# A decoder's expert stage: other blocks of batches, and another pacing of the gathers that merge the experts' outputs

## The chip, the core and the metric

The kernel runs on one core of one Trainium2 chip. The metric is the device time of one execution in microseconds; the median of several executions counts. Engines: TensorE (PE: matrix products and transposes; PEld: its weight loads), VectorE (DVE), ScalarE (ACT), GpSimd (POOL), and SyncE (SP), which here only issues DMAs. GpSimd issues the indirect DMAs (gathers and scatters by row numbers) itself. All DMAs run on the core's 16 DMA engines.

## The reference, cut to what matters

A decoder of two layers over 32 batches of 256 tokens of width 256. Layer 0 and the attention and cross attention of layer 1 come first; the change lies in the last part, the experts of layer 1. Each token is normalised, scored against 8 experts, and gets the sum of its two best experts' outputs, each times its score, added to the residual.

```python
scores = xf @ gate_w + gate_b
topk_s, topk_i = jax.lax.top_k(scores, 2)
comb = zeros.at[arange(n)[:, None], topk_i].add(topk_s)
h = jnp.maximum(einsum('nd,edh->neh', xf, w1) + b1, 0.0)
eo = einsum('neh,ehd->ned', h, w2) + b2
out = einsum('ne,ned->nd', comb, eo)          # then added to the residual x5
```

The kernel computes for each token only its two experts, not all eight.

## The kernel before

The program is a row of phases with a barrier of all engines between them. The last two matter here.

**Cross pass with routing** (`cross_pass`). A software pipeline of slots; in slot n batch n-3 is routed. `file_rows` on GpSimd scatters each normalised row twice into `expert_in`, into the region of its expert. The batches are cut into three blocks (`Dispatch.BLOCKS`: 15, 10 and 7 batches). In each block the rows of one expert are padded to whole tiles of 256 rows, so a block of n batches has 2n + 7 tiles (`Dispatch.tiles`: 37, 27, 21; 85 in all). When the last batch of a block has been routed, DVE makes its tables (`tables`, L2098 to L2139, 20 small operations, each waiting for the one before): which expert and which rows each tile has, and `out_slots`, where each token finds its two results. SP then stores the zero rows of the padding (`pad`). In slots 18, 23, 28 and 33 DVE also makes the low part of a quarter of the expert weights (L2145).

**Expert stage** (`experts_phase`). One tile is 256 rows of one expert. All products are made in fp32r in three passes (high times low, low times high, high times high). For tile m, the loop iteration m on TensorE is: `hT(m)`, transposes of the hidden layer; `xT(m + 2)`, transposes of the input; `up(m + 1)`, the up product, 12 matmuls; `down(m)`, the down product, 12 matmuls. ACT takes the high parts (`x_high`, `h_high`), DVE the low parts and the biases (`x_low` d_xl, `add_b1` d_up, `h_low` d_hl, `add_b2` d_eo). The evacuation d_eo(m) is what DVE does as soon as `down(m)` is done. SP loads d_xs five tiles ahead and stores d_eo into `expert_out` of the block.

**Merging.** When all of a block's tiles are in memory, its batches can be merged. For each batch GpSimd issues four gathers of 128 rows (L2368, d_pick, a ring of four: gather b waits until batch b - 4 is summed), ACT multiplies them by the scores (`weight`, L2393, four operations), DVE adds the two (L2445) and the residual (L2449), and SP stores the result. A gather would otherwise run ahead, so `gather_at` paces the gathers: it counts in halves of a tile, and the gather at half h waits for `up(h // 2)` if h is even, for `down(h // 2)` if it is odd. So there are two gathers a tile and a batch in two tiles; gathers at or behind half 170 (tile 85, the number of tiles) wait for no product. `ready_after` says after which tile a batch's weighting stands in ACT's program; its adds stand one tile later in DVE's, behind that tile's d_eo. Each engine works in the order of its program.

Semaphores count: `xT_psum`, `up_psum` and `out_psum` say how many tiles have their input transposes, up product and down product done; `eo_stored` says what is in memory.

Of the kernel before, what the change touches and what calls it, by code (L numbers as in the profile page):

```python
# [68 lines left out]
def stand_alone(eng, passed):  # L69

    eng.sem_inc(passed, 1)


class Steps:
# [6 lines left out]
    def __init__(self, eng, sem, each, before=0):  # L81
        self.eng, self.sem, self.each, self.before, self.base, self.n = eng, sem, each, before, 0, 0
# [14 lines left out]
def make_identity(nc, tile, ready, before):  # L97

    nc.gpsimd.memset(tile[:, :], 0.0).then_inc(ready, 1)
    nc.gpsimd.wait_ge(ready, before + 1)  # L100
    nc.gpsimd.affine_select(out=tile[:, :], in_=tile[:, :], compare_op=ALU.not_equal, fill=1.0, base=0,
                            pattern=[[-1, P]], channel_multiplier=1).then_inc(ready, 1)
# [1007 lines left out]
class Dispatch:  # L1110


    def __init__(self, nc, ctx, B, S, NE, D):
        T = S // P
        sb = lambda name, shape, dt=F32: ctx.enter_context(nc.sbuf_tensor("e_" + name, shape, dt))
        self.BLOCKS = (B // 2 - 1, B // 4 + 2, B // 4 - 1)
        self.NE, self.TILE = NE, 2 * P
        most = max(self.BLOCKS) * S
        self.region = most + self.TILE
        self.stride = NE * self.region + (NE - 1) * self.TILE  # L1120
        self.tiles = [2 * n * S // self.TILE + NE - 1 for n in self.BLOCKS]
        self.base = [k * self.stride for k in range(len(self.BLOCKS))]
        rows = len(self.BLOCKS) * self.stride
        self.xs_d = nc.dram_tensor("expert_in", (rows, D), F32).ap()
        self.eo_d = [nc.dram_tensor(f"expert_out{k}", (n * self.TILE, D), F32).ap() for k, n in enumerate(self.tiles)]
        self.x5_d = nc.dram_tensor("x5_scratch", (B * S, D), F32).ap()
        self.slots = sb("slots", [P, B, T, 2], I32)
        self.coef = sb("coef", [P, B, T, 2])
        self.ixf, self.pos = sb("ixf", [P, B, T, 2]), sb("pos", [P, B, T, 2])
        self.out_slots = sb("out_slots", [P, B, T, 2], I32)  # L1130
        self.row = [sb(f"row{k}", [P, n], I32) for k, n in enumerate(self.tiles)]
        self.expert = [sb(f"expert{k}", [P, n], I32) for k, n in enumerate(self.tiles)]
# [25 lines left out]
def phase_c(nc, a, x3_d, out, w):  # L1158

    B, S, D = a["ctx_1024"].shape  # L1160
    with ExitStack() as ctx:
        ex = Dispatch(nc, ctx, B, S, a["L1_ffn_gate_w"].shape[1], D)
        x4_d = nc.dram_tensor("x4_scratch", (B * S, D), F32).ap()
        with nc.cleanup_on_exit():
            attention_pass(nc, a, x3_d, x4_d, w)
        nc.all_engine_barrier()
        ex.weights(nc, ctx, a)
        with nc.cleanup_on_exit():
            cross_pass(nc, a, x4_d, w, ex)
        nc.all_engine_barrier()  # L1170
        experts_phase(nc, out, ex, D)
# [1084 lines left out]
def experts_phase(nc, out, ex, D):  # L2256

    NE = ex.NE
    C, T = D // P, ex.TILE // P
    B = sum(ex.BLOCKS)  # L2260
    ROWS = ex.xs_d.shape[0]
    TILES = [(k, j) for k, n in enumerate(ex.tiles) for j in range(n)]
    N = len(TILES)
    XR, ER, GR = 6, 3, 4
    with ExitStack() as ctx:  # L2265
# [20 lines left out]
        xT_psum, xT_high, xT_ready = sem("xT_psum"), sem("xT_high"), sem("xT_ready")  # L2286
        up_psum, up_ready = sem("up_psum"), sem("up_ready")
        hT_psum, hT_high, hT_ready = sem("hT_psum"), sem("hT_high"), sem("hT_ready")
        out_psum, eo_ready = sem("out_psum"), sem("eo_ready")
# [7 lines left out]
        first = [sum(ex.tiles[:k]) for k in range(len(ex.tiles))]  # L2297
        gather_at, pace = [], 0
        for k, n in enumerate(ex.BLOCKS):
            pace = max(pace, 2 * (first[k] + ex.tiles[k] + 1))  # L2300
            for b in range(n):
                gather_at.append(range(pace, pace + 2 * T))
                pace += 2 * T
        ready_after = [min(N, at[-1] // 2 + 2) for at in gather_at]
        merged_after = lambda m: [b for b in range(B) if ready_after[b] == m]

        block = ctx.enter_context(nc.Block())
# [1 line left out]
        @block.sync  # L2309
        def _(sync):  # L2310
            def load(m):
                k, j = TILES[m]
                row = sync.value_load(ex.row[k][0:1, j:j + 1], min_val=0, max_val=ROWS - ex.TILE)  # L2313
                if m >= XR:
                    sync.wait_ge(xT_psum, m - XR + 1)
                sync.dma_start(xs[m % XR][:, :, :], ex.xs_d[bass.ds(row, ex.TILE), :]
                               .rearrange("(t p) d -> p t d", p=P)).then_inc(xs_loaded[m % XR], 16)

            def store(m):
                k, j = TILES[m]  # L2320
                sync.wait_ge(eo_ready, m + 1)
                sync.dma_start(ex.eo_d[k][j * ex.TILE:(j + 1) * ex.TILE, :].rearrange("(t p) d -> p t d", p=P),
                               eo[m % ER][:, :, :]).then_inc(eo_stored[m % ER], 16)

            def load_x5(b):
                if b >= GR:
                    sync.wait_ge(summed, b - GR + 1)
                sync.dma_start(x5[b % GR][:, :, :], x5_rows[b]).then_inc(x5_loaded[b % GR], 16)

            def store_out(b):  # L2330
                sync.wait_ge(summed, b + 1)
                sync.dma_start(out_rows[b], y[b % 2][:, :, :]).then_inc(out_stored[b % 2], 16)

            for m in range(XR - 1):
                load(m)
            for b in range(GR):
                load_x5(b)
            for m in range(N + 1):
                if m + XR - 1 < N:
                    load(m + XR - 1)  # L2340
                if m < N:
                    store(m)
                for b in merged_after(m - 1) + merged_after(N) * (m == N):
                    store_out(b)
                    if b + GR < B:
                        load_x5(b + GR)
            for u in range(2):
                sync.wait_ge(out_stored[u], 16 * (B // 2))

        @block.gpsimd  # L2350
        def _(pool):
            g = nc.gpsimd
            make_identity(nc, ident, consts, 0)
            b = 0
            for k, n in enumerate(ex.BLOCKS):
                done = first[k] + ex.tiles[k]
                for r in range(ER):
                    pool.wait_ge(eo_stored[r], 16 * len([m for m in range(done) if m % ER == r]))
                for _ in range(n):
                    if b >= GR:  # L2360
                        pool.wait_ge(summed, b - GR + 1)
                    stand_alone(pool, pool_passed)
                    for t in range(T):
                        for c in range(2):
                            half = gather_at[b][2 * t + c]
                            if half // 2 < N:
                                pool.wait_ge((up_psum, out_psum)[half % 2], half // 2 + 1)
                            g.indirect_dma_start(pick[b % GR][:, t, c, :], None, ex.eo_d[k],  # L2368
                                                 bass.IndirectOffsetOnAxis(ap=ex.out_slots[:, b, t, c:c + 1], axis=0),
                                                 bounds_check=ex.eo_d[k].shape[0] - 1, oob_is_err=False).then_inc(picked[b % GR], 16)  # L2370
                    b += 1
# [202 lines left out]
```

## Time and profile before

| | us |
|---|---|
| median of 3 runs | 2791.55 |
| lowest, highest | 2788.91, 2796.89 |
| profiled execution | 2796.21 |
| its span, first to last instruction | 2794.4 |
| mean granted TensorE clock, share of full | 0.937 |

The profile is of one execution. A row of the timeline gives start, duration, engine, line, operation, output and inputs, and in brackets how long the engine sat idle before and what ended that. A row of the windows gives start and end, length, each engine's busy time with its count of instructions, then the granted TensorE clock, the busy share of the DMA engines and GB/s. The releaser named by a bracket is inferred: of several waits it is the one that ended last. Matmuls overlap, so their starts are 0.12 us apart though each shows 0.28. Idle time of an engine that nothing waits for costs nothing.

### The profile page before, as it was taken

What the parts mean: (1) busy time and instruction counts of PE and PEld (TensorE: products, weight loads), DVE (VectorE), ACT (ScalarE), POOL (GpSimd) and SP (SyncE); (2) the same over time, 40 slices, a digit from 0 to 9 for tenths busy, and PEclk for the clock granted to TensorE, in tenths of its full rate; (3) what the DMA queues carried; (4) which work ended last, traced back from release to release, by engine and by line L of the source; (5) the groups of instructions that cost most, each with busy time, mean ns of one, the idle gap of its engine ahead of it and who ended that gap; (6) DMA issues with size and microseconds to landing.
All of it is one profiled execution on the core that took longest, in us unless ns stands there. A gap on an engine that the chain in (4) does not pass through costs nothing. (4 is left out here: it accounts for less than half of the span.)

```text
span 2794.4 us, 49866 instructions
## 1 busy us (share of the span) xinstructions
PE 2401.1 (86%) x16388; PEld 1884.8 (67%) x16388; DVE 1893.6 (68%) x4393; ACT 1515.3 (54%) x3016; POOL 1359.5 (49%) x1313
## 2 busy tenths in 40 slices
PE   5999999479999668999999999887998987799991
PEld 3666666369999645656656566555887776799981
DVE  3888888456565347777777777754777775567773
ACT  3777777345555336776767676662433432223443
POOL 4677777444443254554545545402665555002556
PEclk9999999789999878999999999997999998899996
DMA  2222221252121001111111111114332433445885
GB/s 66 66 77 61 76 76 50 60 146 96 66 74 52 25 18 37 37 42 41 41 41 38 43 43 37 33 35 137 102 121 99 155 111 108 156 139 186 256 249 179
DMA packets 234395, 242.72 MB, mean 87 GB/s; under 512 B 34670, under 2 KB 220272, under 8 KB 233888
## 3 DMA queue, kind: packets, MB, share of 16 engines
q1 hardware_dynamic: 212576, 193.14, 22.6%
q0 software_dynamic: 20480, 46.39, 5.5%
q8 instruction: 138, 2.26, 0.4%
q14 instruction: 113, 0.93, 0.2%
q10 hardware_dynamic: 1088, 0.00, 0.0%
HBM read 133.82 MB, written 101.25 MB: 84 GB/s over the span
## 5 line engine op out<-in xcount | busy, mean ns | idle before, releaser
L1527 DVE TENSOR_REDUCE f_nm<-f_raw 128x4 f32<-128x1024 f32 x256 | 312.8, 1222 | 108.5 <-PE f_raw L1641 105.7
L1353 POOL TENSOR_TENSOR f_hm<-f_hm,f_mhalf 128x64 f32<-128x64 f32 x32 | 366.4, 11449 | 2.7
L1420 ACT ACTIVATE f_PT<-f_sco 128x1024 f32<-128x1024 f32 x256 | 262.2, 1024 | 97.3 <-PE f_sco L1658 97.2
L2368 POOL DMA_INDIRECT d_pick<-expert_out,e_out_slots x128 | 141.0, 1102 | 255.4 <-DMA expert_out<-d_eo 154.4
L910 ACT ACTIVATE b_hT<-b_H,b_b1r 128x512 f32<-128x512 f32 x128 | 88.2, 689 | 163.5 <-PE b_H L1039 148.1
L1658 PE MATMUL f_sco<-f_q4T,f_k4T 64*128 64x256 f32 x1024 | 130.6, 335 | 50.1 <-DMA f_q4T<-f_nmT 35.6
L2387 ACT ACTIVATE d_hh<-d_H 128x512 fp32r<-128x512 f32 x85 | 50.8, 598 | 205.2 <-PE d_H L2473 205.2
L1895 POOL DMA_INDIRECT expert_in<-g_xm,e_slots x128 | 131.0, 1024 | 40.2 <-issue 37.0
L677 PE MATMUL a_bank<-a_w,a_xnT 128*128 128x512 f32 x256 | 127.0, 620 | 21.9 <-ACT a_xnT L394 21.9
L1054 PE MATMUL b_O<-b_w2l,b_hTh 128*128 128x256 f32 x512 | 144.9, 283 | 0.0
L1054 PE MATMUL b_O<-b_w2h,b_hTl 128*128 128x256 f32 x512 | 144.7, 283 | 0.0
L1054 PE MATMUL b_O<-b_w2h,b_hTh 128*128 128x256 f32 x512 | 144.7, 283 | 0.0
L864 POOL DMA_INDIRECT x_scratch<-b_y,b_idx x64 | 69.2, 1082 | 144.6 <-DVE b_y L987 128.7
L1658 PEld LDWEIGHTS f_sco<-f_q4T,f_k4T 64*128 64x128 f32 x1024 | 82.4, 198 | 84.6 <-DMA f_q4T<-f_nmT 42.6
L1641 PE MATMUL f_raw<-f_k4T,f_q4T 64*128 64x256 f32 x1024 | 131.3, 336 | 6.9 <-DVE f_nm L1527 5.2
L1351 POOL TENSOR_SCALAR f_hm<-f_hm 128x64 f32<-128x64 f32 x32 | 32.4, 1014 | 204.4 <-DVE f_hm L1491 204.4
L972 DVE TENSOR_TENSOR b_hTl<-b_hT,b_hTh 128x512 fp32r<-128x512 f32 x128 | 88.2, 690 | 61.4 <-ACT b_hTh L912 57.5
L1641 PEld LDWEIGHTS f_raw<-f_k4T,f_q4T 64*128 64x128 f32 x1024 | 81.7, 197 | 56.0 <-issue 41.2
L2493 PE MATMUL d_O<-e_w2l,d_hh 128*128 x340 | 98.4, 289 | 13.5 <-DVE d_hl L2430 13.5
L1344 POOL TENSOR_SCALAR f_rs<-f_mv 128x2 f32<-128x2 f32 x32 | 7.0, 220 | 205.8 <-DVE f_mv L1477 205.8
L1039 PE MATMUL b_H<-b_xTh,b_w1l 128*128 128x512 f32 x256 | 102.5, 400 | 2.5 <-DVE b_xTl L957 2.5
L2493 PE MATMUL d_U<-e_w1l,d_xh 128*128 x340 | 104.0, 306 | 0.1
(367 smaller groups left out, 7758.8 us busy)
## 6 DMA issues: line engine op xcount, KB each, us to landing
d_xs<-expert_in SPq DMA_DIRECT2D x85, 256.0 KB
expert_out<-d_eo SPq DMA_DIRECT2D x85, 256.0 KB
x_scratch<-a_x SPq DMA_DIRECT2D x64, 256.0 KB, 2.2
b_w<-in_L_ffn_W_dram SPq DMA_DIRECT2D x16, 1024.0 KB
a_x<-in_x_dram SPq DMA_DIRECT2D x32, 256.0 KB
a_cx<-in_ctx_dram SPq DMA_DIRECT2D x32, 256.0 KB
f_x<-x_scratch SPq DMA_DIRECT2D x32, 256.0 KB
f_q4T<-f_nmT SPq DMA_DIRECT2D x128, 64.0 KB, 2.3
```

Of the source, the lines that this page charges most:

```text
L677: last = t_.matmul(bank_of(part)[:, :], xnT[b % 2][:, c, t * P:(t + 1) * P], w[:, c, 0:2 * D], start=c == 0, stop=c == C - 1)
L910: s.activation(hT[f % 4][:, :], HB[f % 4][:, :], ACT.Gelu, bias=b1r[:, e, f:f + 1], scale=RATIO).then_inc(hidden, 1)
L1039: last = t_.matmul(HB[f % 4][:, :], w[e % 2][:, c, cols], x[:, c, :], start=m == 0, stop=m == len(products) - 1)
L1054: last = t_.matmul(OB[t // 2][:, t % 2 * D:(t % 2 + 1) * D], h[:, f, cols], w[e % 2][:, f, :], start=f == 0 and m == 0, stop=f == FC - 1 a ...
L1353: g.tensor_tensor(hm[b % 2][:, :], hm[b % 2][:, :], mhalf[:, :], ALU.pow).then_inc(hroot, 1)
L1420: s.activation(PT[n % 3][:, t, :, :], heads(SCO), ACT.Exp, scale=float(DH) ** -0.5).then_inc(probs_ready, 1)
L1527: v.tensor_reduce(nm[:, t, g * HG:(g + 1) * HG], heads(RAW), AX.X, ALU.max, negate=True)\
L1641: last = t_.matmul(heads(RAW)[:, place(h), :], q4T[b % 3][at, h // 2, t * P:(t + 1) * P], k4T[b % 3][at, h // 2, :], start=True, stop=True)
L1658: last = t_.matmul(heads(SCO)[:, place(h), :], k4T[b % 3][at, h // 2, t * P:(t + 1) * P], q4T[b % 3][at, h // 2, :], start=True, stop=True)
L1895: g.indirect_dma_start(ex.xs_d, bass.IndirectOffsetOnAxis(ap=ex.slots[:, b, t, k:k + 1], axis=0), xm[b % 3][:, t, :], None, bounds_check=e ...
L2368: g.indirect_dma_start(pick[b % GR][:, t, c, :], None, ex.eo_d[k], bass.IndirectOffsetOnAxis(ap=ex.out_slots[:, b, t, c:c + 1], axis=0), b ...
L2493: last = t_.matmul(halves(bank)[:, t, :], x[:, c, t * P:(t + 1) * P], y_[:, bass.ds(e, 1), c, :].rearrange("p o d -> p (o d)"), start=c == ...
```

## The change

The blocks become 18, 9 and 5 batches, with 43, 25 and 17 tiles, again 85. The pacing counts in sixths of a tile. In block 0 gathers are two sixths apart, three a tile, so a batch takes 4/3 of a tile; in the other blocks three sixths apart, two a tile, as before. The first sixths of tile m now wait for `xT(m + 2)`, the middle ones for `up(m + 1)`, the last for `down(m)`: all three are of loop iteration m. From tile 84 on there is no wait for a product. Block 0's gathers begin at tile 44 (before: at half 76, tile 38), block 1's at tile 69, and block 2's follow when the last tile is stored. All line numbers behind L2297 grow by one.

```diff
-        self.BLOCKS = (B // 2 - 1, B // 4 + 2, B // 4 - 1)
+        self.BLOCKS = (B // 2 + 2, B // 4 + 1, B // 8 + 1)
...
         for k, n in enumerate(ex.BLOCKS):
-            pace = max(pace, 2 * (first[k] + ex.tiles[k] + 1))
+            each = 2 if k == 0 else 3
+            pace = max(pace, 6 * (first[k] + ex.tiles[k] + 1))
             for b in range(n):
-                gather_at.append(range(pace, pace + 2 * T))
-                pace += 2 * T
-        ready_after = [min(N, at[-1] // 2 + 2) for at in gather_at]
+                gather_at.append(range(pace, pace + 2 * T * each, each))
+                pace += 2 * T * each
+        ready_after = [min(N, at[-1] // 6 + 2) for at in gather_at]
...
-                            half = gather_at[b][2 * t + c]
-                            if half // 2 < N:
-                                pool.wait_ge((up_psum, out_psum)[half % 2], half // 2 + 1)
+                            m, sixth = divmod(gather_at[b][2 * t + c], 6)
+                            if m + 1 < N:
+                                pool.wait_ge(*((xT_psum, min(N, m + 3)), (up_psum, m + 2), (out_psum, m + 1))[sixth // 2])
```

The start of the gathers in GpSimd's program, before. Semaphores are shown here under the names of earlier phases that used the same ones: a_dve_passed is `up_psum`, a_bank_full2 `out_psum`, a_cx_loaded1 `xT_psum`, a_bank_taken4 `summed`; a_cx_loaded0, a_x_loaded2 and a_x_loaded3 are the three `eo_stored`.

```order
L2368 DMA d_pick0<-expert_out0,e_out_slots 128x256 [waits a_cx_loaded0,a_x_loaded2,a_x_loaded3,a_dve_passed]
L2368 DMA d_pick0<-expert_out0,e_out_slots 128x256 [waits a_bank_full2]
L2368 DMA d_pick0<-expert_out0,e_out_slots 128x256 [waits a_dve_passed]
L2368 DMA d_pick0<-expert_out0,e_out_slots 128x256 [waits a_bank_full2]
L2368 DMA d_pick1<-expert_out0,e_out_slots 128x256 [waits a_dve_passed]
```

The same place after:

```order
L2369 DMA d_pick0<-expert_out0,e_out_slots 128x256 [waits a_cx_loaded0,a_x_loaded2,a_x_loaded3,a_cx_loaded1]
L2369 DMA d_pick0<-expert_out0,e_out_slots 128x256 [waits a_dve_passed]
L2369 DMA d_pick0<-expert_out0,e_out_slots 128x256 [waits a_bank_full2]
L2369 DMA d_pick0<-expert_out0,e_out_slots 128x256 [waits a_cx_loaded1]
L2369 DMA d_pick1<-expert_out0,e_out_slots 128x256 [waits a_dve_passed]
```

The two waits that took turns have become three.

GpSimd's last waits for a product, before: block 1 (expert_out1) gives way to block 2 (expert_out2), which goes on for seven batches.

```order
L2368 DMA d_pick3<-expert_out1,e_out_slots 128x256 [waits a_bank_taken4,a_dve_passed]
L2368 DMA d_pick3<-expert_out1,e_out_slots 128x256 [waits a_bank_full2]
L2368 DMA d_pick3<-expert_out1,e_out_slots 128x256 x2
L2368 DMA d_pick0<-expert_out1,e_out_slots 128x256 [waits a_bank_taken4]
L2368 DMA d_pick0<-expert_out1,e_out_slots 128x256 x3
L2368 DMA d_pick1<-expert_out2,e_out_slots 128x256 [waits a_bank_taken4,a_cx_loaded0,a_x_loaded2,a_x_loaded3]
L2368 DMA d_pick1<-expert_out2,e_out_slots 128x256 x3
```

After, with five batches of block 2 behind it:

```order
L2369 DMA d_pick1<-expert_out1,e_out_slots 128x256 [waits a_bank_taken4,a_cx_loaded1]
L2369 DMA d_pick1<-expert_out1,e_out_slots 128x256 [waits a_dve_passed]
L2369 DMA d_pick1<-expert_out1,e_out_slots 128x256 x2
L2369 DMA d_pick2<-expert_out1,e_out_slots 128x256 [waits a_bank_taken4]
L2369 DMA d_pick2<-expert_out1,e_out_slots 128x256 x3
L2369 DMA d_pick3<-expert_out2,e_out_slots 128x256 [waits a_bank_taken4,a_cx_loaded0,a_x_loaded2,a_x_loaded3]
L2369 DMA d_pick3<-expert_out2,e_out_slots 128x256 x3
```

The last wait for a product is now for an up product, and 26 gathers follow it instead of 34.

DVE while block 0 is merged, before: the adds of one batch, then a tile without any.

```order
L2438 TENSOR_TENSOR d_eo1<-d_O0,e_b2 128x512
L2445 TENSOR_TENSOR d_y0<-d_pick2 128x512
L2449 TENSOR_TENSOR d_y0<-d_y0,d_x52 128x512
L2430 SCALAR_TENSOR_TENSOR d_hl1<-d_H1,d_hh1 128x512
L2414 TENSOR_TENSOR d_xl1<-d_T1,d_xh1 128x512
L2421 TENSOR_LOAD e_expert1
L2421 ISA x2
L2425 ISA
L2425 TENSOR_TENSOR d_up0<-d_U0,e_b1 128x512
L2438 REGISTER_ALU
L2438 TENSOR_TENSOR d_eo2<-d_O1,e_b2 128x512
L2430 SCALAR_TENSOR_TENSOR d_hl0<-d_H0,d_hh0 128x512
```

After, in block 0: the adds of the next batch follow in the next tile, three tiles of four.

```order
L2439 TENSOR_TENSOR d_eo1<-d_O0,e_b2 128x512
L2446 TENSOR_TENSOR d_y1<-d_pick1 128x512
L2450 TENSOR_TENSOR d_y1<-d_y1,d_x51 128x512
L2431 SCALAR_TENSOR_TENSOR d_hl0<-d_H0,d_hh0 128x512
L2415 TENSOR_TENSOR d_xl0<-d_T0,d_xh0 128x512
L2422 TENSOR_LOAD e_expert1
L2422 ISA x2
L2426 ISA
L2426 TENSOR_TENSOR d_up1<-d_U1,e_b1 128x512
L2439 REGISTER_ALU
L2439 TENSOR_TENSOR d_eo2<-d_O0,e_b2 128x512
L2446 TENSOR_TENSOR d_y0<-d_pick2 128x512
```

The adds stand in iterations 48 to 70 (three of four) and then in 73, 75, 77, 79, 81 and 83; before, in 42, 44 and so on up to 84.

## Rows read from the trace of the kernel before

**Rows 1.** The page's head: span, and busy time, share and instructions by engine.

```profile
span 2794.4 us, 49866 instructions
PE 2401.1 (86%) x16388; PEld 1884.8 (67%) x16388; DVE 1893.6 (68%) x4393; ACT 1515.3 (54%) x3016; POOL 1359.5 (49%) x1313
```

**Rows 2.** Windows of the expert stage: PE, PEld, DVE, ACT, POOL; clock, DMA share, GB/s.

```profile
2400.00:2540.00 140.00, 139.99 (x1177) 138.16 (x1175) 97.92 (x147) 40.22 (x74) 0.00 (x0) 1.00 0.45 138
2564.34:2722.36 158.02, 147.37 (x1217) 143.13 (x1216) 122.51 (x191) 72.45 (x153) 85.64 (x76) 1.00 0.82 252
2740.85:2786.69 45.84, 0.00 (x0) 0.00 (x0) 11.97 (x18) 13.63 (x32) 35.77 (x34) 0.52 0.63 189
```

**Rows 3.** The chain that ended last, in order of time: start, duration, what.

```profile
2748.42 0.30 issue
...
2785.57 3.00 DMA d_pick<-expert_out,e_out_slots
...
2791.13 0.69 DVE d_y L2449
```

**Rows 4.** Timeline of GpSimd: block 0's first gather, two beside a merge, the train's first.

```profile
2544.67 1.08 POOL L2368 DMA_INDIRECT d_pick<-expert_out,e_out_slots  x1 [154.37 <-DMA expert_out<-d_eo]
...
2572.63 1.52 POOL L2368 DMA_INDIRECT d_pick<-expert_out,e_out_slots  x1 [1.44 <-PE d_O L2493]
2574.45 1.00 POOL L2368 DMA_INDIRECT d_pick<-expert_out,e_out_slots  x1 [0.30 <-issue]
...
2739.03 1.52 POOL L2368 DMA_INDIRECT d_pick<-expert_out,e_out_slots  x1 [1.33 <-PE d_O L2493]
```

**Rows 5.** Timeline of DVE: evacuations of tiles 36, 42, 44, 45, 46, 82 and 84.

```profile
2540.90 0.69 DVE L2438 TENSOR_TENSOR d_eo<-d_O,e_b 128x512 f32<-128x512 f32 x1 [0.64 <-PE d_O L2493]
...
2563.68 0.69 DVE L2438 TENSOR_TENSOR d_eo<-d_O,e_b 128x512 f32<-128x512 f32 x1 [0.51 <-PE d_O L2493]
...
2571.99 0.69 DVE L2438 TENSOR_TENSOR d_eo<-d_O,e_b 128x512 f32<-128x512 f32 x1 [0.73 <-PE d_O L2493]
...
2576.56 0.69 DVE L2438 TENSOR_TENSOR d_eo<-d_O,e_b 128x512 f32<-128x512 f32 x1 [0.76 <-PE d_O L2493]
...
2580.30 0.69 DVE L2438 TENSOR_TENSOR d_eo<-d_O,e_b 128x512 f32<-128x512 f32 x1 [0.73 <-PE d_O L2493]
...
2730.18 0.69 DVE L2438 TENSOR_TENSOR d_eo<-d_O,e_b 128x512 f32<-128x512 f32 x1 [0.73 <-PE d_O L2493]
...
2738.38 0.69 DVE L2438 TENSOR_TENSOR d_eo<-d_O,e_b 128x512 f32<-128x512 f32 x1 [1.96 <-PE d_O L2493]
```

**Rows 6.** Timeline of TensorE: the last matmul of the up product of tile 83.

```profile
2728.33 0.28 PE L2493 MATMUL d_U<-e_w1h,d_xh 128*128 x1
```

**Rows 7.** Timeline of ACT: the wait behind a weighting, and the latest weighting.

```profile
2576.91 0.60 ACT L2387 ACTIVATE d_hh<-d_H 128x512 fp32r<-128x512 f32 x1 [1.26 <-PE d_H L2473]
...
2691.37 1.71 ACT L2393 ACTIVATE d_pick<-d_pick,e_coef 128x256 f32<-128x256 f32 x4 [1.45 <-issue]
```

**Rows 8.** Windows: one tile, and one pair of tiles, columns as in rows 2.

```profile
2577.20:2581.36 4.16, 4.16 (x38) 4.16 (x37) 3.09 (x6) 1.51 (x4) 2.41 (x3) 1.00 0.98 331
...
2593.84:2602.16 8.32, 7.73 (x66) 7.53 (x66) 6.45 (x11) 3.75 (x9) 4.51 (x5) 1.00 0.84 259
```

**Rows 9.** Windows: slots of the cross pass, columns as in rows 2.

```profile
2118.59:2131.51 12.92, 12.32 (x77) 10.55 (x77) 9.92 (x39) 7.09 (x15) 7.91 (x11) 1.00 0.32 99
2131.51:2155.42 23.91, 14.68 (x77) 12.68 (x77) 18.61 (x61) 5.32 (x14) 8.40 (x11) 0.79 0.16 56
...
2208.36:2223.97 15.61, 13.68 (x77) 11.75 (x77) 11.62 (x41) 5.44 (x14) 9.52 (x11) 0.89 0.26 85
2275.74:2298.76 23.02, 14.64 (x77) 12.61 (x77) 17.71 (x62) 5.21 (x14) 8.40 (x11) 0.78 0.18 58
2311.67:2328.18 16.51, 14.00 (x77) 11.74 (x77) 10.04 (x40) 5.48 (x14) 8.53 (x11) 0.90 0.63 218
```

**Rows 10.** The tile g_mine: durations in ns (min/median/max), first and last start, forms.

```profile
L2132 DVE TENSOR_TENSOR g_mine<-g_iota,e_ixf x3: 392/493/660, 2137.4 to 2380.4; 128x480 f32<-128x480 f32 x1, 128x320 f32<-128x320 f32 x1, 128x224 f32<-128x224 f32 x1
```

## What was predicted

> **What bounds the kernel now.** I read the page first: TensorE is busy 86% of 2794.4 us [rows 1], but that is an average over stages, and the change touches only the last stage (the experts, from about 2390 us) and, slightly, the routing work before it. So the next view is the table of windows inside the expert stage [rows 2]. Until tile 37 no gather runs and TensorE never idles. Then come some 158 us in which each tile also carries gathers and merges: the tile takes 4.16 us, the DMA engines are 82% busy. Then come 46 us with no matmul at all, GpSimd busy 36 of 46. The chain that ended last says what these are: a train of gathers, each about 1.0 us plus 0.30 us of issue, the last at 2785.57, then its landing, its weighting and its two adds, the last of which starts at 2791.13 [rows 3]. So the end is set by how many gathers are left when TensorE stops, and by when the train may start.
>
> **The tail, term one.** The plan before paces two gathers a tile, so 35 gathers run unhindered from 2739.03, the first released by the last down product [rows 4]. 34 gaps fill 2785.57 - 2739.03 = 46.54 us, 1.369 us each (the 1.30 of most, and some of 1.8). The new plan leaves 6 of block 1's gathers and 20 of block 2's without a wait, and the last one with a wait is released by up(84), not by down(84). That is a train of 27, with 26 gaps: 26 x 1.369 = 35.6 us.
>
> **Where the train starts, term two.** The DVE rows give the tile time [rows 5]. From the evacuation of tile 36 at 2540.90 to that of tile 42 at 2563.68: 3.80 us a tile without a merge. With a merge after it, the next evacuation comes 4.57 us later (2571.99 to 2576.56), and the one after 3.74 later (2580.30), 8.31 a pair. This closes: 21 pairs x 8.32 = 174.7 = 2738.38 - 2563.68. The chain in a merge tile is evacuation, two adds, the low half of the hidden layer, down product, evacuation; nothing in it depends on the tile before having no merge, so I take 4.57 for each merge tile in a row. The order shows in which iterations merges stand: 48 to 70, three of four (18), then 73, 75 .. 83 (6). From tile 42 on: 6 x 3.80 = 22.8; six groups of four, 6 x (3 x 4.57 + 3.74) = 104.7; one of 3.80; then 6 x 4.57 + 5 x 3.74 = 46.1. Evacuation 84 starts at 2563.7 + 22.8 + 104.7 + 3.8 + 46.1 = 2741.1, 2.7 later than now. Evacuation 83 is then at 2736.5. Where no merge intervenes, an up product ends 1.57 before the evacuation of the same iteration (2728.33 + 0.28 to 2730.18 [rows 5, 6]), and a released gather starts 0.65 after the evacuation of the releasing product (2739.03 against 2738.38), the evacuation itself 0.1 after the product. So the train starts at 2736.5 - 1.57 + 0.75 = 2735.7 and its last gather at 2735.7 + 35.6 = 2771.3: 14.3 us earlier than 2785.57. What follows it is unchanged.
>
> Can block 2's gathers go on at once? They wait for the last expert output in memory. Tile 36 was evacuated at 2540.90 and the gather waiting for its store started at 2544.67 [rows 4, 5]: 3.77. So not before 2741.1 + 3.8 = 2744.9; the seven gathers ahead of them fill until 2735.7 + 7 x 1.37 = 2745.3. Covered, by 0.4 us only; a landing 2 us later costs 2.
>
> **The dense stretch, term three.** For 24 tiles (44 to 68) three gathers go with each tile, and 18 batches in all are merged. I test each resource over four tiles, 17.45 us by the sum above.
> GpSimd: 12 gathers x 1.30 (2572.63 + 1.52 + 0.30 = 2574.45 is the row with the pitch; without the long one it is 1.30) = 15.6, plus 0.52 for each gather that meets a merge, 3 x 0.52: 17.2 [rows 4]. It fits with 1% to spare.
> The Trainium skill, SBUF - State Buffer, "Who interferes with whom", infers that a tensor_tensor, even with both inputs in SBUF, does not hold up descriptor generation; by that GpSimd would need only 15.6 of 17.45 and this term would be nothing. The trace disagrees: the gather issued together with the merge's first add takes 1.52 against 1.00.
> ACT and DVE: the weighting before the merge is late at times, and yet after the largest gap, 1.45 us ahead of the one at 2691.37, the pair still takes 8.3; and after a late one ACT still sat idle 1.26 before its next TensorE wait [rows 7]. A landing 1 to 2 us later than now is free, more is not.
> DMA: a tile moves 0.52 MB (256 KB in, 256 KB out), a batch 1.05 MB (four gathers of 128 KB, x5, output). Four tiles: 2.10 + 3.15 = 5.24 MB in 17.45 us, 300 GB/s. Now it is 252 on average, 259 over one pair, and 331 within one tile at 98% busy [rows 2, 8]. At 331 the tile would be 3.96 us, under 4.36, cost nothing. At 259 it would be 5.06, 0.70 above, times 24 = 16.8 us. That is the range of this term, 0 to 16.8. I take 2 us, near the low end, because the tiles in which the DMA engines run 98% busy at 331 do not come out longer than others, and because the ends of late weightings are still covered.
> On this the Trainium skill, DMA: Bandwidth & Descriptors, "Latency and other measured facts", speaks against the change: memory latency rises from 0.2 us to 2 us at high load. That would be 2 us more on each landing; the gathers' cover above would take most of it. No row here separates it.
>
> **The routing work, term four.** The tables of a block are made on DVE when its last batch is routed: now after batches 14, 24, 31, then after 17, 26, 31. Now the first two fall into the same slot as a split of the expert weights: 23.91 and 23.02 us against 12.92 for a plain slot; a split alone makes 15.61, so 2.69 [rows 9]. The tables alone are then 23.91 - 12.92 - 2.69 = 8.3 and 7.4, and since DVE is serial they cost that wherever they stand. Block 0's grow by a fifth: three operations of 0.66 us at 480 elements [rows 10] become some 0.13 longer each, other operations a few hundredths, in all +0.6; blocks 1 and 2 shrink by about 0.1 and 0.25. Parted from the split, the clock, at 0.79 in that slot, might fall twice instead of once, up to 1 us each. The zero rows of block 1 are stored two slots later; the slot they fall in now takes 16.51, so up to 3.6 may be saved. I take +0.5, range -3.6 to +3.
>
> **Sum.** -14.3 + 2 + 0.5 = -11.8 us. The profiled execution took 2796.21 (its span 2794.4 and 1.8 around it), so 2784.4 on its scale; the median of the runs is 2791.55, 4.7 lower, so **2780 us**.
>
> **Rivals.**
> (1) The stretch costs nothing and block 1's zero rows leave a busy slot: -14.3, to -17.4 at best; 2774 to 2777. For it: pairs of 8.3 us whatever the DMA load. Chance 0.15.
> (2) GpSimd is the bound in the stretch: its 17.2 leave 1%; each release that comes after it is ready adds to it. If six of twelve gathers meet an add instead of three, four tiles need 15.6 + 3.1 = 18.7, 4.68 a tile, 0.32 x 24 = 7.6 us more; the gain is 14.3 - 7.6 - 0.5 = 6.2, 2785. A last store that lands 2 us late adds 2 to it, 2787. Chance 0.20.
> (3) The DMA engines are the bound: the burst of 331 can't be held, and the stretch runs at the rate seen over pairs. At 259 GB/s, +16.8; at 252, 5.20 a tile and +20.2. Then -14.3 + 20.2 + 0.5 = +6.4, slower than before, 2798. It decides from a mean tile of 4.36 + 13.8 / 24 = 4.93 us. Against it: the 331 row, and the stores and loads of SP are spread over time once three merges fall in four tiles. Chance 0.10.
> (4) The change doing nothing would need the tail to keep its length; the waits are taken out in the program, so I give that no chance of its own.
>
> **How the numbers follow.** Forecast 0.55, with its own range 2776 to 2784; rivals 0.15, 0.20, 0.10. Range: from rival 1's 2773 to 2789, which leaves out most of rival 3 and the outer edge of rival 1, some 0.15. A measurement of this kernel can tell 0.3%, 8.4 us, from no change. Faster by more: nearly all of the forecast, rival 1 and a fifth of rival 2, 0.72. Within: the rest of rival 2 and half of rival 3, 0.22. Slower: 0.06.
>
> **What would show it.** After: the last evacuation near 2741 to 2744 (start of the expert stage unmoved), 27 gathers in a train from about 2736, the last near 2771 to 2774; evacuations 4.57 apart in merge tiles between tiles 48 and 71. Wrong if those are over 4.9 apart on average, if ACT waits for d_pick in front of late evacuations (rival 3), if GpSimd never idles between tiles 45 and 68 (rival 2), or if the train breaks before block 2's first gather.

## The result, and the profile after

| | us |
|---|---|
| after: median of 6 runs (2800.06 to 2811.4) | 2806.84 |
| before: median of 6 runs (3 of them those given above) | 2793.47 |
| ratio as recorded, 95% interval | 1.0031 [1.0016, 1.0045] |
| profiled execution of after, its span | 2808.18, 2806.4 |
| predicted | 2780, 2773 to 2789 |

Slower, where faster was forecast; the two medians alone give 1.0048. The page's head of after, the same lines as [rows 1]:

```profile
span 2806.4 us, 49866 instructions
PE 2411.6 (86%) x16388; PEld 1887.1 (67%) x16388; DVE 1891.9 (67%) x4393; ACT 1513.5 (54%) x3016; POOL 1353.7 (48%) x1313
```

Windows of after, columns as in [rows 2]: twenty tiles (48 to 67) of the dense stretch, by which the tiles with three gathers each are meant; tiles 69 to 84; and the tail.

```profile
2592.12:2692.79 100.67, 87.35 (x640) 76.74 (x640) 70.08 (x111) 45.50 (x100) 59.83 (x60) 1.00 0.85 256
2697.24:2767.16 69.92, 60.22 (x491) 57.85 (x489) 50.84 (x79) 29.07 (x62) 35.87 (x34) 1.00 0.76 229
2767.16:2797.44 30.28, 0.00 (x0) 0.00 (x0) 9.38 (x14) 10.22 (x24) 22.56 (x22) 0.55 0.69 202
```

The first row is twenty tiles of 5.03 us, where 4.36 on average was forecast. No engine fills it: PE is busy 87%, GpSimd 60 of 101 us, the DMA engines 85%. One tile of it shows the wait: GpSimd's three gathers, TensorE's last matmul of the up product, and DVE.

```profile
2632.35 1.00 POOL L2369 DMA_INDIRECT d_pick<-expert_out,e_out_slots  x1 [1.45 <-PE d_O L2494]
2633.65 1.00 POOL L2369 DMA_INDIRECT d_pick<-expert_out,e_out_slots  x1 [0.30 <-issue]
2634.95 0.99 POOL L2369 DMA_INDIRECT d_pick<-expert_out,e_out_slots  x1 [0.30 <-issue]
...
2634.90 0.28 PE L2494 MATMUL d_U<-e_w1h,d_xh 128*128 x1
...
2636.75 0.69 DVE L2426 TENSOR_TENSOR d_up<-d_U,e_b 128x512 f32<-128x512 f32 x1 [1.66 <-PE d_U L2494]
```

The up product ends at 2634.90 + 0.28 = 2635.18, and TensorE goes on with the down product. DVE has sat idle and has nothing left to wait for but `up_psum`, yet d_up begins at 2636.75, 1.57 later. In the trace's list of semaphore events the increment stands at 2636.61, 1.43 us behind that end; DVE passes its wait at 2636.64, and GpSimd, which waits for the same count, at 2636.64 too. So the waiters did not sleep: the count was late (the end of a matmul is modelled by the profiler, but the next product's matmuls follow it at their usual pace). It is so in every tile from 46 to 68 (by 1.27 to 1.56 us), while in the tiles ahead of them an increment stands within 0.02 us of the matmul's end. d_up late makes the transposes of the hidden layer late, and they every later step: 5.03 a tile.

The tail did as planned. GpSimd's first and last gather of the train, and the last evacuation:

```profile
2761.57 0.99 POOL L2369 DMA_INDIRECT d_pick<-expert_out,e_out_slots  x1 [1.70 <-PE d_U L2494]
...
2797.44 1.13 POOL L2369 DMA_INDIRECT d_pick<-expert_out,e_out_slots  x1 [0.31 <-issue]
...
2767.16 0.69 DVE L2439 TENSOR_TENSOR d_eo<-d_O,e_b 128x512 f32<-128x512 f32 x1 [1.96 <-issue]
```

From evacuation 84 to the last gather it is 30.28 us, against 47.19 [rows 3, 5].

### The profile page after: what moved, and what is told of

Read it like the earlier page. It is cut to its first block and busy times, and to the rows that moved or that the text cites. A ratio compares the mean times of both kernels' runs of the same rounds, so it can differ in the third digit from the quotient of the medians.

```text
span 2806.4 us, 49866 instructions
## 1 busy us (share of the span) xinstructions
PE 2411.6 (86%) x16388; PEld 1887.1 (67%) x16388; DVE 1891.9 (67%) x4393; ACT 1513.5 (54%) x3016; POOL 1353.7 (48%) x1313
## 5 line engine op out<-in xcount | busy, mean ns | idle before, releaser
L2369 POOL DMA_INDIRECT d_pick<-expert_out,e_out_slots x128 | 131.4, 1027 | 272.3 <-PE d_T L2474 209.0
```

## The experiments

Two quantities are read from each trace: the **expert stage**, from DVE's first d_eo to the end of the span (390.8 us in the trace of before, 396.1 in that of after), and the **dense tile**, the mean spacing of evacuations 45 to 68 (4.14 and 5.00). Ratios are against runs of the kernel before in the same session. A session is one sitting on one chip, in which several kernels run in turn; a trace is of one execution. The runs lie in nine sessions, the first of them that of the result above. The first trace of before, taken ahead of the forecast, is counted with it; whether it was the same session isn't on record.

**Blocks alone.**

```diff
-        self.BLOCKS = (B // 2 - 1, B // 4 + 2, B // 4 - 1)
+        self.BLOCKS = (B // 2 + 2, B // 4 + 1, B // 8 + 1)
```

> The kernel before with the new blocks (18, 9 and 5 batches) alone: two gathers a tile everywhere, released by up and down products as before. It tells the cost of the blocks in the routing work apart from the pacing, and the trace of the dense stretch from its cause. Block 0's gathers begin at tile 44, 82 have a wait and 46 have none, so the train at the end has 46 gaps of 1.369 us less one, 61.6 us, against 46.5 before. Merges begin three pairs later, so evacuation 84 comes 3 x 0.83 = 2.5 us sooner. Theory A (the expert stage of the changed kernel began 6.6 us later because of the tables and the zero rows): evacuation 1 near 2414, last gather near 2804, time near 2812 us. Theory B (it was an accident of one execution): evacuation 1 near 2408, time near 2806 us. Both theories on the dense stretch expect pairs of tiles of 8.3 us here and counts of TensorE seen 0.1 us after its last matmul.

2812.76, ratio 1.0087 [1.0068, 1.0107]. Evacuation 1 at 2407.2, last gather 2799.34, dense tile 4.12. Theory B holds for the start of the stage: the blocks alone do not put it off (from the attention pass to the first d_xl 525.0 us, as in before; see term four below). The time is 7 us above theory B's: the attention pass took 841.8 us here against 835.2 in before (below).

**Release points alone**, at two a tile: after's code, with before's blocks and

```diff
-            each = 2 if k == 0 else 3
+            each = 3
```

> The changed kernel with the blocks of before (15, 10, 7) and two gathers a tile in all blocks, three sixths apart: released by the input transposes and by the up product in turn, instead of by up and down. Theory U (GpSimd's waiting for the up product, the count that VectorE waits for too, is what made d_up begin 1.5 us late in the dense stretch): tiles with a gather under way at the up product's end take near 5.0 us, evacuation 84 comes 20 us or more later than before, time above 2810 us. Theory D (three gathers a tile are what makes it late): d_up begins within 0.5 us of the up product's end, pairs of tiles 8.3 us, time 2790 to 2797. In the changed kernel tiles 69 to 84, released in this way at two a tile, took 4.42 us on average instead of 4.16: if that is the points' price and not the blocks', 47 x 0.26 = 12 us, time near 2805.

2785.24, 0.9987 [0.9975, 0.9998]; again in another session 2787.45, 0.9988 [0.9978, 0.9998]. Dense tile 4.14, stage 386.4. Theory U falls at this density (in such a session; see below), and the points are worth 4 to 5 us of the stage (387.0 in the second trace): the train begins earlier.

**Three a tile, all released by down(m).**

```diff
-   pool.wait_ge(*((xT_psum, min(N, m + 3)), (up_psum, m + 2), (out_psum, m + 1))[sixth // 2])
+   pool.wait_ge(out_psum, m + 1)
```

> The changed kernel, but all gathers of tile m wait for down(m): in the dense stretch three a tile as in the changed kernel, and no gather waits for the input transposes or for the up product. Theory U (the wait for the up product): d_up begins within 0.5 us of the up product's end again, tiles of 4.4 to 4.6 us in the stretch, evacuation 84 near 2750, the last gather near 2782, time 2783 to 2793. Theory D (three gathers a tile, one of them under way when the up product ends): tiles stay at 5.0, time 2800 to 2810.

2789.70, 0.9991 [0.9977, 1.0005]; dense tile 4.35, stage 380.3 (381.6 and 0.9988 [0.9973, 1.0002] in another session). It looked like theory U was right. In the trace a gather was under way as the up product ended (GpSimd, TensorE, DVE), as in the late tile above, and d_up followed in 0.3 us:

```profile
2632.09 1.00 POOL L2369 DMA_INDIRECT d_pick<-expert_out,e_out_slots  x1 [0.30 <-issue]
...
2632.04 0.28 PE L2494 MATMUL d_U<-e_w1h,d_xh 128*128 x1
...
2632.61 0.69 DVE L2426 TENSOR_TENSOR d_up<-d_U,e_b 128x512 f32<-128x512 f32 x1 [0.19 <-issue]
```

**The up product's gathers left out, its wait kept.** In batches 4 to 17 GpSimd passes the wait and then issues no gather, and ACT waits for as many landings fewer. This kernel's output lacks these expert rows.

```diff
+        issued = lambda b: [not GR <= b < ex.BLOCKS[0] or at % 6 // 2 != 1 for at in gather_at[b]]
...
+                            if not issued(b)[2 * t + c]:
+                                continue
```

> The changed kernel with every gather that the up product releases left out in batches 4 to 17 (the wait stays in GpSimd's program, the rows of d_pick keep what an earlier batch left), so two gathers a tile in tiles 50 to 68 with the same three waits. Its output lacks these expert rows. Theory U (the wait for the up product delays d_up): tiles stay near 5.0 us, time within 3 us of the changed kernel. Theory D (the third gather does): tiles fall to a mean of 4.36 us, 19 x 0.67 = 12.7 us less than the changed kernel, near 2794.

2783.11, 0.9978 [0.9969, 0.9988]; dense tile 4.30. That looked like theory D's. But tiles 46 to 48 still had three gathers and the wait, and took 3.77 us each, as tiles without gathers do. Both answers made sense only if the changed kernel itself behaved otherwise here, so it was run again, beside two more releases.

**The changed kernel again.**

> The changed kernel, unchanged, once more beside the others. The single trace of it shows d_up 1.4 to 1.7 us late in every tile from 46 to 68, while neither two gathers a tile with these waits nor three a tile without them showed it. Theory P (a property of the program: three gathers a tile together with the wait for the up product): tiles of 5.0 us between 46 and 68 again, 22 us from evacuation 42 to 84 above before, time 2800 to 2808. Theory C (something of that one execution or chip): tiles of 4.36 us, time 2780 to 2790.

2785.74, 0.9981 [0.9968, 0.9994]: theory C. Dense tile 4.32, stage 378.4. The windows of this trace: tiles 46 to 68, tiles 70 to 84, and the tail.

```profile
2577.05:2676.32 99.27, 91.27 (x738) 87.14 (x737) 78.06 (x122) 52.32 (x114) 74.44 (x68) 1.00 0.93 292
2680.89:2744.12 63.23, 56.48 (x459) 54.10 (x457) 47.15 (x73) 26.43 (x56) 33.50 (x32) 1.00 0.79 239
2744.12:2774.84 30.72, 0.00 (x0) 0.00 (x0) 9.08 (x14) 10.22 (x24) 23.11 (x22) 0.57 0.66 199
```

The same program moves 292 GB/s where it moved 256. So the 256 of the first trace, so near to the 259 on which a rival rested, was not a limit of the DMA engines: it goes with the longer tiles.

**Without the up product's wait, without the transposes' wait.** The three semaphores become (xT, xT, down), and (down of the tile before, up, down).

> The changed kernel, but the middle gather of each three waits for the input transposes, as the first does, and none for the up product. Theory U2 (at three a tile it is the wait for the up product that makes d_up late): tiles of 4.36 us on average between 46 and 68, evacuation 84 23 us after what the changed kernel shows less its start, last gather 25 us less, time 2780 to 2790. Theory X (any release spread over the tile, so that a gather's wait ends inside it, does it): tiles stay at 5.0, time 2800 to 2808.

> The changed kernel, but the first gather of each three waits for the down product of the tile before instead of the input transposes that follow it at once; the middle one still waits for the up product. Theory U2: tiles stay at 5.0 us between 46 and 68 with d_up over 1.3 us late, time 2798 to 2808. Theory T (it is the wait for the transposes, whose count SyncE and ScalarE wait for too): 4.36 us, time 2780 to 2790.

2784.18, 0.9977 [0.9964, 0.9990] (in another session 0.9992 [0.9979, 1.0006]) and 2786.88, 0.9993 [0.9979, 1.0008]; dense tiles 4.34 and 4.31, stages 378.6 and 378.5. As the changed kernel had no delay here either, they tell nothing of its cause, and neither do the two runs of three a tile released by down(m).

**More sessions, and the layout.** The kernel before again (2790.28, 1.0000 [0.999, 1.001] against its other runs) and the changed one a third time, together; then the changed one a fourth time, with a variant of before in which only the size of a region in memory is changed:

```diff
-        most = max(self.BLOCKS) * S
+        most = (B // 2 + 2) * S
```

> The changed kernel, unchanged, a third time, in five rounds beside before. Theory C1 (the late d_up of tiles 46 to 68 belongs to the one session in which it was first measured): tiles of 4.32 us there, 378 us from the first evacuation to the end, time 0.2 to 0.5% under before. Theory C2 (it comes and goes from session to session, or from execution to execution): tiles of 5.0 us and 396 us again, or single executions above 2800 among those below 2795.

> The changed kernel, unchanged, in one more session, beside the runs of before. Theory C1 (the late d_up of tiles 46 to 68 belongs to the first session): tiles of 4.3 us there, 378.4 us from the first evacuation to the end, and with an attention pass of 908 us a time of 2785 to 2789. Theory C2: tiles of 5.0 us, 396 us, time above 2800.

> The kernel before with nothing changed but the size of an expert's region in expert_in, as the new blocks need it (18 batches instead of 15), so that the tensors in memory lie as in the changed kernel. In four traces the attention pass, whose code the change does not touch, took 905 to 908 us with the new blocks and 898.3 us in all three traces with the old ones, which took 8 to 10 us off the gain. Theory M (where the tensors lie in memory sets it): attention pass near 905 to 908 us here, time 2797 to 2800, 0.25 to 0.35% above before. Theory N (it is not the layout): 898 us, time as before, 2788 to 2792.

(This expectation counts the attention pass over a stretch some 63 us longer than the rows shown below do.)

The third: 2788.59, 0.9995 [0.9983, 1.0007], dense tile 4.30, stage 378.5 beside 391.4 of before. The fourth: **2811.30**, 1.0042 [1.0029, 1.0055], dense tile 5.09, stage 398.7. So theory C2: the late counts come and go from session to session. They are not bound to one chip: the session of 2785.74 and that of 2811.30 carry the same chip number. The layout's variant, in the late session: 2800.08, 0.9997 [0.9985, 1.0010], dense tile 4.14, stage 389.7. Two gathers a tile ran without a late count in a session in which three had them; so did before in the first session. Still, a late session costs before something outside its expert stage: its medians there are 2793.5, 2798.9 and 2796.6 us, and 2788.1 to 2790.3 in the other six. Its first trace and that of the layout's variant take 532.1 and 532.8 us from the attention pass to the first d_xl, its second trace 525.3. The page says which kind a session was, by two issues of SP and the time to their landing, its last number. After in the first session, then in the one without late counts:

```profile
d_xs<-expert_in SPq DMA_DIRECT2D x85, 256.0 KB
expert_out<-d_eo SPq DMA_DIRECT2D x85, 256.0 KB
```

```profile
d_xs<-expert_in SPq DMA_DIRECT2D x85, 256.0 KB, 3.5
expert_out<-d_eo SPq DMA_DIRECT2D x85, 256.0 KB, 2.6
```

In the 15 traces without late counts both rows have a time to landing, and the traces hold 29,670 to 29,980 semaphore events. In the five of the late sessions, for before as for after, the rows have none, and the traces hold 24,080 to 24,800: events are missing, 4,500 to 5,100 of them landings of DMAs. TensorE's counts are among the others, in tiles with gathers. But a missing event is not a late count: in the changed kernel's two late traces those of the hidden layer's transposes are missing in 17 and in all 23 of the tiles 46 to 68, and ACT follows the transposes in 0.04 us in each of them, while the up product's count is recorded, and late. In the first trace of before the up product's is missing in every second tile from 45 to 83, and d_up is on time there.

**A version to beat both**: blocks of 19, 9 and 4, three a tile in every block, released by down(m).

```diff
+        self.BLOCKS = (B // 2 + 3, B // 4 + 1, B // 8)
...
+            each = 2
...
+                pool.wait_ge(out_psum, m + 1)
```

> A version to beat both: blocks of 19, 9 and 4 batches (45, 25 and 15 tiles), three gathers a tile in every block, all released by down products. In the trace with 18, 9 and 5 and the same release the expert stage (first evacuation to end) took 380.3 us against 390.7 before. Four more batches are merged while TensorE works, 4 x 0.83 = 3.3 us; the train at the end begins with the last store's landing, 3.8 us after evacuation 84, and has 16 gathers, 15 x 1.369 = 20.5, so its last starts 24.3 us after evacuation 84 instead of 32.3, 8.0 less. Net 4.7 less: expert stage near 375.6 us, time near 2778. Against it: if GpSimd or the DMA engines can't hold three a tile for 37 tiles, tiles grow beyond 4.4 and up to 5.0 us, time 2790 to 2800.

2775.01 (4 runs), 0.9949 [0.9929, 0.9968]: the fastest of all, stage 376.2. Its attention pass was short as well, 830.5 us; the stage alone is 15 us shorter than before's. And again, in a session that turned out late:

> The version of 19, 9 and 4 batches with all gathers released by down products, once more. In a session without late counts: 376 us from the first evacuation to the end and 0.5% under before, as in the first measurement. In a session with them (before near 2799): theory U2 (the wait for the up product is needed for the delay): tiles of 4.4 us from 50 on, 376 us, 0.5% under before, near 2785. Theory D (density is enough): 5.0 us a tile from 47 on, 37 tiles x 0.6 = 22 us more, 398 us, time near 2807, above before.

2803.19, 1.0028 [1.0015, 1.0041], stage 400.8, dense tile 4.91: theory D. No gather waits for an up product here, so the wait for it is not the condition. Here the delay is not the same in every tile: the up product's count is 2.6 to 3.0 us late in every fourth tile from 55 to 83. One tile (GpSimd, ACT, TensorE's last up matmul, DVE):

```profile
2610.49 1.01 POOL L2369 DMA_INDIRECT d_pick<-expert_out,e_out_slots  x1 [0.48 <-issue]
2611.80 0.99 POOL L2369 DMA_INDIRECT d_pick<-expert_out,e_out_slots  x1 [0.30 <-issue]
2613.10 1.00 POOL L2369 DMA_INDIRECT d_pick<-expert_out,e_out_slots  x1 [0.30 <-issue]
...
2611.91 0.60 ACT L2388 ACTIVATE d_hh<-d_H 128x512 fp32r<-128x512 f32 x1 [3.08 <-DMA x_scratch<-g_y]
...
2611.71 0.28 PE L2494 MATMUL d_U<-e_w1h,d_xh 128*128 x1
...
2615.05 0.69 DVE L2426 TENSOR_TENSOR d_up<-d_U,e_b 128x512 f32<-128x512 f32 x1 [0.31 <-DMA g_cx<-in_ctx_dram]
```

d_up begins 3.06 us after the up product's end (2611.99), and the increment stands 2.93 behind it. The hidden layer's transposes ended at 2610.12; ACT's d_hh, which has nothing else left to wait for, begins at 2611.91, and the increment stands at 2611.89. So counts for other waiters are late as well. The releasers in the brackets (a DMA of the cross pass) are false: with events missing, the trace can't name them.

**Both densities in one kernel** (three a tile for nine batches, then two):

> The changed kernel with three gathers a tile for batches 0 to 8 only (tiles 44 to 55) and two a tile for all others. In a session without late counts: 4.4 us a tile to 57, then pairs of 8.3; 18 batches end at tile 74, so about 12 gathers more are left for the end than in the changed kernel: 12 x 1.369 = 16.4 us, fewer merges before (6 x 0.83 = 5 us) taken off: 378.4 + 11.4 = 390 us from the first evacuation, time near before's. In a session with them: theory D: 5.0 us a tile from 46 to 56 and 8.3 a pair behind; theory W: 5.0 us a tile all along to 74.

No late session: 2790.45, 1.0007 [0.9991, 1.0023], stage 386.5 (expected 390). The kernel with gathers left out, a second time, also ran without late counts (2786.30, 0.9994 [0.9983, 1.0004], stage 379.9).

## Why the prediction was wrong

**Tail, term one: right.** 26 gaps filled 35.87 us (forecast 35.6), and 36.26, 37.01 and 35.59 in the other three traces.

**Start of the train, term two: right.** It begins 5.5 to 5.6 us ahead of evacuation 84 in three traces (forecast 5.4) and 6.8 in the third, whose last tile took 5.81 us instead of 4.57. From evacuation 42 to 84 the second trace has 178.4 us, forecast 177.4 without term three. One thing was off: block 2's first gather starts 4.5 to 4.8 us after evacuation 84, not 3.8, so GpSimd stood idle ahead of it for 1.21 us in the second trace and 1.32 in the first, instead of 0.30. The cover of 0.4 was too thin, at a price of some 0.9 us that the sum did not hold (it is within the 36.26).

**Dense stretch, term three: here it failed, and by session.** Without late counts it costs 1.0 us in the second trace and 1.8 in the third (forecast 2). In the first session it is 197.0 - 177.4 = 19.6 us, outside its range of 0 to 16.8, some 2 of them in tiles 69 to 84, whose mean was 4.35 instead of the second trace's 4.21. The step that failed is the list of resources that the forecast tested for this stretch: GpSimd, ACT and DVE, DMA engines. Each held. What gave way was not on it: the time from the end of a TensorE product until the engines that wait see its count. In the trace of before d_up follows the up product in some 0.15 us in most tiles where DVE is free, and the forecast took it for a constant. Neither rival 2 (GpSimd sat idle 1.45 in each tile) nor rival 3 (d_up, the step that came late, needs no gather, the trace names no wait of ACT for d_pick, and the DMA engines moved 256 GB/s at 85% where 292 at 93% was to be had; there ACT waited for a landing three times, 1.0 us in all) was the mechanism. That rival 3's place, price and threshold (over 4.93 us a tile, 2798) came near is luck.

**Routing work, term four: right in some traces, exceeded in others.** From the attention pass's last row-maximum to the first d_xl it is 525.3 us in the new trace of before and 525.7 in the second of after, +0.4 (forecast +0.5). Rows of DVE in these two:

```profile
L1527 DVE TENSOR_REDUCE f_nm<-f_raw x256: 1191/1225/1227, 1028.7 to 1863.9; 128x4 f32<-128x1024 f32 x128
L2414 DVE TENSOR_TENSOR d_xl<-d_T,d_xh x85: 678/680/693, 2389.2 to 2722.0; 128x512 fp32r<-128x512 f32 x85
```

```profile
L1527 DVE TENSOR_REDUCE f_nm<-f_raw x256: 1192/1225/1226, 1028.2 to 1871.3; 128x4 f32<-128x1024 f32 x128
L2415 DVE TENSOR_TENSOR d_xl<-d_T,d_xh x85: 679/681/692, 2397.0 to 2733.9; 128x512 fp32r<-128x512 f32 x85
```

Without late counts the old blocks' three traces take 525.0 to 525.3, and 18, 9 and 5 take 525.0 to 525.7 in six traces of eleven, but 528.9 to 531.0 in the other five, 4 to 6 us more, which is outside the forecast's range of -3.6 to +3. In those five TensorE's clock was granted at its low level for 97 to 104 us of this stretch, in the six for 89 to 96. The forecast had thought of the clock, at up to 1 us for each fall; what decides between the two kinds isn't shown. In the first session the stage of after began 6.6 us later than before's: 2.2 of them arose ahead of the attention pass, 0.8 in it, 1.5 from there to the first d_xl and 2.1 from there to the first evacuation.

**What was not in the sum.** Where no count is late, the stage is 13.0 us shorter (391.4 to 378.4; forecast 12.3), but the medians gained only 4.5 and 1.1. The same rows show where most of it went: the attention pass, whose code is the same, takes 835.2 us (1028.7 to 1863.9) before and 843.1 after. Over all traces it takes 832 to 836 with the old blocks (five), 833 to 845 with 18, 9 and 5 (thirteen; the changed kernel 836.0, 843.1, 843.3, 844.8), and 831 and 832 with 19, 9 and 4. The layout alone had 836.3. One program can have both: three a tile by down(m) took 844.2 and 833.3. Its long pass has 101 us at the low level of TensorE's clock and its short one 68, but before's new trace has 94 in 835.2 us, so the clock is at most a part of it. What makes the pass longer stays open, and so does whether the new blocks have a share in it. The forecast carried an unchanged part over as a constant, with no spread.

**What stays open.** That late counts belong to the session, three of the nine, is shown by one program at 2785.7, 2788.6, 2806.8 and 2811.3 us: none of its runs in the first two of these sessions is above 2797.6, and none in the other two below 2800.1. That three gathers a tile bring them out in such a session and two of the old pacing, which follow each other in pairs behind a down product [rows 4], do not is seen in five traces (two each of the changed kernel and of the old pacing, one of 19, 9 and 4). Two a tile with the new release points was never measured in one; tiles 69 to 84 of the changed kernel suggest a small price, since `out_psum` was late there by 0.7 us in four tiles. What a session has or lacks isn't shown. The missing events make the recording of the counts a suspect. The Trainium skill, NOTIFIC — the notification-queue block, "Overflow: three behaviours, one of which stalls the engine", says that records are dropped when a queue is full in one mode, and that inside the block the sources are held back. The late traces have something like each, over 5,000 events fewer and counts 1.4 us late, and not on the same counts; that the two belong together is a guess. No run here parts the recording from the chip, since the span of every execution comes from its recording.

## What to carry to other kernels

When each engine and the DMA engines have room and a step still waits, compare the end of the last matmul with the start of its waiter: if the gap grows from 0.3 to 1.6 us though the waiter is idle and has no other wait, the count itself is late, and no engine's busy share shows it. Before explaining a result by its one trace, measure the same program in a second session: here that was worth 20 us, more than the whole change. And a gain of 0.5% of the time in one stage needs to be held against what the untouched stages do from execution to execution: here the attention pass alone lay between 831 and 845 us.

## What was not expected of the hardware

Counts of TensorE reached two waiting engines 1.3 to 1.6 us after the matmul's end in 23 tiles in a row, and up to 3.9 us in the version with 19, 9 and 4 batches, while TensorE went on with its next product.

The forecast charged 1.52 us instead of 1.00 for each gather beside a merge's add. That holds only for a gather that starts while the add is under way: in all twenty traces it takes 1.00 plus what is left of the add, less some 0.13. A gather that has begun before the add stays at 1.00, and so do some that start within 0.04 us of it. After's first trace has one of each, the add here being d_y:

```profile
2637.37 0.99 POOL L2369 DMA_INDIRECT d_pick<-expert_out,e_out_slots  x1 [1.42 <-PE d_O L2494]
...
2637.95 0.68 DVE L2446 TENSOR_TENSOR d_y<-d_pick 128x512 f32<-128x512 f32 x1
...
2698.56 0.69 DVE L2450 TENSOR_TENSOR d_y<-d_y,d_x 128x512 f32<-128x512 f32 x1
...
2698.75 1.37 POOL L2369 DMA_INDIRECT d_pick<-expert_out,e_out_slots  x1 [3.65 <-PE d_T L2474]
```

In the second the add has 0.50 left when the gather starts, and the gather takes 0.37 more. In the late tiles GpSimd paid nothing for the merges, which is one more sign against rival 2.
